# Quantised attention: turned weights as levels by VectorE, and the value products with a constant column left out

## What is computed

```
def _fq(x, delta, zp, n_bits):
    xi = _round_ste(x / delta) + zp
    xq = jnp.clip(xi, 0.0, 2.0 ** n_bits - 1.0)
    return (xq - zp) * delta

def _attn(x, ctx, wq, wk, wv, wo, bo, dq, dk, dv, dw):
    q, k, v = ...                       # x @ wq, ctx @ wk, ctx @ wv, split into heads
    sim = jnp.einsum('bhid,bhjd->bhij', _fq(q, dq, 128.0, 8), _fq(k, dk, 128.0, 8)) * SCALE
    attn = jax.nn.softmax(sim, axis=-1)
    out = jnp.einsum('bhij,bhjd->bhid', _fq(attn, dw, 0.0, 8), _fq(v, dv, 128.0, 8))
    return out.transpose(0, 2, 1, 3).reshape(b, n, D) @ wo + bo

h1 = _ln(x, ln1_g, ln1_b)
x = _attn(h1, h1, a1_wq, ..., d_w1) + x
h2 = _ln(x, ln2_g, ln2_b)
x = _attn(h2, context, a2_wq, ..., d_w2) + x
h3 = _ln(x, ln3_g, ln3_b)
a, g = jnp.split(h3 @ ff_w1 + ff_b1, 2, axis=-1)
x = a * jax.nn.gelu(g, approximate=False) @ ff_w2 + ff_b2 + x
```

## Time and profile before

| | |
|---|---|
| median of 3 runs | 2011.68 us (2011.1 to 2012.37) |
| profiled execution | 2007.97 us |
| its span | 2006.2 us |
| PE busy | 1808.6 us, 90% of the span |
| PE weight loads busy (beside PE) | 1344.1 us, 67% |
| DVE busy | 1237.6 us, 62% |
| ACT busy | 1074.7 us, 54% |
| POOL busy | 905.3 us, 45% |
| mean granted clock of PE | 0.933 |

### The profile page before, as it was taken

The page is one execution under the profiler, slowest core; times in us unless marked ns, Lnnn a source line. Parts: engine busy times, 40 slices in busy tenths (PEclk is TensorE's granted clock), DMA queues, the critical chain, the costliest instruction groups (busy, mean ns, idle before and its releaser), DMA issues.

```text
span 2006.2 us, 34807 instructions
## 1 busy us (share of the span) xinstructions
PE 1808.6 (90%) x12481; PEld 1344.1 (67%) x12481; DVE 1237.6 (62%) x2220; ACT 1074.7 (54%) x3142; POOL 905.3 (45%) x1209
## 2 busy tenths in 40 slices
PE   4998988789799889889999999999999999999997
PEld 4887876466566656657667677676676676766766
DVE  5899995744654464463575665865746647365471
ACT  2232225665575475565575564655645656565662
POOL 4466554654463363363254443644444333333340
PEclk8999998788878878879999999999999999999999
DMA  7200000002000000000002000000000000000000
GB/s 226 92 11 6 11 6 6 1 7 90 1 6 6 1 6 6 0 6 7 1 7 90 1 7 6 7 7 1 7 6 2 12 1 7 22 7 1 12 1 11
DMA packets 31073, 35.66 MB, mean 18 GB/s; under 512 B 3164, under 2 KB 29752, under 8 KB 30520
## 3 DMA queue, kind: packets, MB, share of 16 engines
q1 hardware_dynamic: 30904, 33.44, 5.2%
HBM read 31.34 MB, written 2.10 MB: 17 GB/s over the span
## 4 chain that ended last, share of the span: by engine, by line
PE 61%; DVE 17%; ACT 10%; issue 6%; POOL 2%; SPq 2%; DMA 1%; DVEq 0%; POOLq 0%; ACTq 0%
PE ps L594 33%; PE ps L806 6%; PE ps L744 6%; PE ps L816 5%; PE ps L850 4%; ACT work L983 3%; ACT work L990 3%; DVE work L1183 3%; DVE xn L1037 2%; PE ps L607 2%; DVE rowmax L1187 2%; PE ps L831 2%; ACT hT L899 1%; PE ps L766 1%; POOL work L1376 1%
## 5 line engine op out<-in xcount | busy, mean ns | idle before, releaser
L594 PE MATMUL ps<-hT,w_slot 128*128 128x256 f32 x1696 | 410.1, 396 | 17.1 <-ACT hT L899 16.1
L1300 POOL TENSOR_TENSOR work<-KT,own_head 128x512 f32<-128x512 f32 x256 | 262.4, 1046 | 285.4 <-PE ps L806 179.9
L594 PEld LDWEIGHTS ps<-hT,w_slot 128*128 128x128 f32 x1696 | 323.5, 196 | 77.2 <-ACT hT L899 21.7
L990 ACT ACTIVATE work<-work,rowmax 128x128 f32<-128x128 f32 x768 | 244.9, 391 | 167.8 <-DVE rowmax L1187 167.0
L816 PEld LDWEIGHTS ps<-ident,work 128*128 128x128 f32 x1536 | 200.1, 153 | 170.0 <-issue 90.4
L983 ACT ACTIVATE work<-ps,rowmax,score_scale 128x128 f32<-128x128 f32 x512 | 229.3, 484 | 118.7 <-DVE rowmax L1191 118.3
L816 PE MATMUL ps<-ident,work 128*128 128x128 f32 x1536 | 266.4, 302 | 17.9 <-ACT work L990 17.0
L806 PE MATMUL ps<-work,QT 128*128 128x512 f32 x512 | 266.4, 605 | 10.0 <-POOL work L1300 4.9
L1376 POOL TENSOR_SCALAR work<-work,winv 128x128 f32<-128x128 f32 x512 | 185.0, 382 | 167.7 <-DVE winv L1203 165.3
L1217 DVE RECIPROCAL O<-ps 128x128 f32<-128x128 f32 x128 | 122.3, 955 | 174.6 <-PE ps L850 173.9
L976 ACT ACTIVATE work<-ps 128x512 f32<-128x512 f32 x256 | 150.7, 596 | 91.4 <-PE ps L816 91.2
(11 more groups left out here) (131 smaller groups left out, 3170.3 us busy)
## 6 DMA issues: line engine op xcount, KB each, us to landing
ctx_in<-in_ctx SPq DMA_DIRECT2D x32, 256.0 KB, 2.7
w_slot<-in_L_xattn_W SPq DMA_DIRECT2D x2, 1024.0 KB, 6.2
w_slot<-in_L_xattn_ff_w SPq DMA_DIRECT2D x1, 2048.0 KB, 11.5
w_slot<-in_L_xattn_ffn_w SPq DMA_DIRECT2D x2, 1024.0 KB, 9.8
w_slot<-in_L_xattn_w SPq DMA_DIRECT2D x2, 1024.0 KB, 10.0
out<-x_all SPq DMA_DIRECT2D x8, 256.0 KB, 2.1
x_all<-in_x SPq DMA_DIRECT2D x1, 1536.0 KB, 11.4
pad<-in_mask_Bx1x1xS_fk SPq DMA_DIRECT2D x1, 1024.0 KB, 7.6
```

Of the source, the lines that this page charges most:

```text
L594: mm = pe.matmul(dst, lhsT(k), rhs(k), start=(k == 0 and not onto), stop=(k == chunks - 1 and not more))
L990: ex = act.activation(prob[i % NPF][:, tok(h)], src[:, tok(h)], ACT.Exp, bias=shifts[:, at:at + 1])
L1300: pool.tensor_tensor(KB[u % NK].rearrange("p (h k) -> p h k", h=HU), keys, own_head[:, e:HC:2].unsqueeze(2).broadcast_to([P, HU, S]), ALU. ...
```

## The change

The copy of a turned tile goes from ACT's queue to DVE's, and computes another thing: `min(x, MAGIC + 255) - MAGIC`, the level itself and not its complement. With levels the products with the constant column are not needed, so `values` has four products instead of eight, and `out_scale` has no minus sign. The two constants `top` and `below` go with their two memsets at the start. ACT's steps in the quantised phase now hold exponentials alone; nothing in the other layers changes.

```diff
@@ -823,13 +821,12 @@ values(u), PE
-                    for n in range(4):
+                    for e in range(2):
                         for x in range(2):
-                            pair, e = u % UJ * 2 + x, n % 2
+                            pair = u % UJ * 2 + x
                             at = pair % 4 * 32
-                            rhs = below[:, :].broadcast_to([P, S]) if n < 2 else PTb[u % 2][:, tok(2 * x + e)]
-                            mm = pe.matmul(bank(4 + j)[at:at + 32, m * S:(m + 1) * S], Vzb[st][:, j, pair, 2 * e:2 * e + 2, :], rhs,
-                                           start=(n == 0), stop=(n == 3))
+                            mm = pe.matmul(bank(4 + j)[at:at + 32, m * S:(m + 1) * S], Vzb[st][:, j, pair, 2 * e:2 * e + 2, :],
+                                           PTb[u % 2][:, tok(2 * x + e)], start=(e == 0), stop=(e == 1))
                     mm.then_inc(s["o_ps"], 1)
@@ -964,16 +961,11 @@ step(i), ACT
-                    if 0 <= u < U:
-
-                        act.wait_ge(s["o_ps"], U * ap + u + 1 - (2 if quant else 4))
+                    if not quant and 0 <= u < U:
+
+                        act.wait_ge(s["o_ps"], U * ap + u + 1 - 4)
                         act.wait_ge(s["PT_ps"], U * ap + u + 1)
-
-                        if quant:
-
-                            act.activation(PTb[u % 2], bank(2 + u % 2), ACT.Relu, bias=top[:, 0:1], scale=-1.0).then_inc(s["PT_ready"], 1)
-                        else:
-                            act.activation(PTF[u % 4], bank(2 + u % 2), ACT.Copy).then_inc(s["PT_ready"], 1)
+                        act.activation(PTF[u % 4], bank(2 + u % 2), ACT.Copy).then_inc(s["PT_ready"], 1)
@@ -1203,6 +1195,12 @@ DVE
+                def levels(u):
+
+                    dve.wait_ge(s["o_ps"], U * ap + u + 1 - 2)
+                    dve.wait_ge(s["PT_ps"], U * ap + u + 1)
+                    dve.tensor_scalar(PTb[u % 2], bank(2 + u % 2), MAGIC + 255.0, MAGIC, ALU.min, ALU.subtract).then_inc(s["PT_ready"], 1)
+
@@ -1223,6 +1221,8 @@ step(i), DVE
                     if quant and 0 <= i - SUM_LAG < U and (i - SUM_LAG) % 2:
                         inverses((i - SUM_LAG) // 2)
+                    if quant and 0 <= i - lag < U:
+                        levels(i - lag)
 
                     u = i - lag - 1
                     if quant and 0 <= u < U and u % UJ == UJ - 1:
@@ -1250,7 +1250,7 @@ tables(), DVE
-                    dve.tensor_scalar(out_scale[:, n:n + 1], deltas[:, 4 * n + 2:4 * n + 3], deltas[:, 4 * n + 3:4 * n + 4], -1.0,
+                    dve.tensor_scalar(out_scale[:, n:n + 1], deltas[:, 4 * n + 2:4 * n + 3], deltas[:, 4 * n + 3:4 * n + 4], 1.0,
```

More of the change, by code:

```diff
@@ L304, in program @@
         winv = sb("winv", [P, 2, 2 * HU])
-        top = sb("top", [P, 1])
-        below = sb("below", [P, 1], BF16)
         oinv = [[o[:, n // 2, n % 2 * P:(n % 2 + 1) * P] for n in range(U // 2)] for o in O]
@@ L1404, in _ @@
             pool.memset(neg_half[:, :], -0.5)
-            pool.memset(top[:, :], MAGIC + 255.0)
-            pool.memset(below[:, :], -255.0)
             pool.memset(ones_pair[:, 0:4:3, :], 1.0)
```

## The result

The changed kernel takes 2016.39 us (median of 8 runs, 2015.19 to 2017.62). In the same comparison the kernel before takes 2010.22 us (8 runs, 2007.16 to 2013.53). The ratio is 1.0031, with a 95% interval from 1.0021 to 1.0042, so the change costs about 6 us. The forecast was 2022 us, 10 us above the runs shown and 10.8 by the sum: the direction came, in a bit more than half the size.

The account below looks back on a forecast made before the run. PE was busiest but taken not to bound the close handovers, where VectorE is late. Eight pairs of +1.96 (close) and -0.61 us (network) give +10.8 us, so a median of 2022 us, range 2004 to 2032.

Parts of the forecast that it names:

- The close handover: Where the next phase's keys, queries and values come during this phase's last tiles (eight of 16): VectorE's queue adds 1.7 us.
- the 7.72 us gap: VectorE's idle time before the addition into x_all, after the network: tile 7's copy falls into it and adds nothing.
- The output products: Behind each close handover: clock down more often after the longer wait, 0 to 1.2 us, taken as 0.25.
- the worst case: Rival: clock falls at every close handover ahead of the output products, 1.2 instead of 0.25 us; 2030 us, chance 0.12.
- the copies of tiles 4 and 5: Close handover, before Q's and V's first operations: copies fill VectorE's idle gaps; 0.1 us, bounds 0 to 0.4.
- tile 0's before xn: Copy of tile 0 just ahead of xn on VectorE, in all 16 phases: 0 to 0.21 us, taken as 0.1.
- the low tiles: Tiles 1 and 2, at PE's low clock: omitted value products save 0.19 us a phase, the lower bound of 0.19 to 0.38.
- The phases with the network behind: The eight phases followed by a feed-forward network: 0.1 us added, 0.71 saved by omitted products, -0.61 us each.
- PE bounds the layer: Rival: the 19.5 us of omitted products come through, close handovers cost only the excess over PE's work; 1999 us, chance 0.14.
- No change: Rival: right signs, wrong sizes; a handover costs 0.8 instead of 1.8 us, low tiles credited fully; 2012 us, chance 0.17.
- The copy of 0.43 us: Rival, the skill's first rule: VectorE's copy takes 0.43 instead of 0.75 us, sum 5.7 us; 2017 us, chance 0.04.
- ScalarE's relief: 128 copies of 0.688 us leaving ScalarE, costed at nothing; 0.01 given to faster for an unseen effect.

Follow-up runs that it names:

- e3c: Changed kernel with the copies of tiles 6 and 7 back on ScalarE (no cap at 255) in the eight close phases only; 1997.90 us, 0.9943 of before.
- e4: Changed kernel with one more VectorE copy, into a spare buffer, ahead of tile 7's copy in the eight close phases; 2025.32 us, 1.0080 of before.
- e5: Changed kernel with one more VectorE copy ahead of tile 7's copy in the eight phases with the network behind; 2015.46 us, 1.0027 of before.
- e8: Changed kernel with four unused products on PE before tile 6's value products in the eight close phases; 2012.50 us, 1.0013 of before.
- e2: Kernel before with only the copy moved to VectorE, all eight products a tile kept; 2019.61 us, 1.0055 of before.
- e2b: Second run, for another profile, of the kernel before with only the copy moved to VectorE, eight products kept; 2016.10 us, 1.0038 of before.
- e1: Changed kernel with all copies back on ScalarE as levels (no cap at 255), four products a tile; 2001.32 us, 0.9960 of before.
- e3: Changed kernel with the copies of tiles 6 and 7 back on ScalarE (no cap at 255) in every phase; 1999.67 us, 0.9951 of before.
- e7: Changed kernel with eight unused products on PE before tile 6's value products in the eight close phases; 2022.79 us, 1.0064 of before.
- e6: Tiles 0 to 3 as in the changed kernel, tiles 4 to 7 as before (ScalarE complements, eight products), cap kept everywhere; 2001.67 us, 0.9957 of before.

## Why the prediction was right, and where not

**Its mechanism held.** The close handover is lost to two copies in DVE's queue between V's quantising and OT. I gave that 1.7 us; V's third to OT grew by 1.57, and OT to the exponential by 0.04. e3c removes it and e4 adds to it one for one. e5 shows that the same copy elsewhere costs nothing, as the 7.72 us gap said.

**The output products were under-sized.** I took 0.25 us of a range from 0 to 1.2. The piece from the first exponential to the turn of xn grew by 0.51. The prediction took the duration 2.90 of the earlier trace rows for a likely one; the trace has 3.10 to 3.78. Within the eight phases the piece follows it: with output products of 3.10 us it took 9.87 (nothing lost), with 3.68 us 10.60. So up to about 3.1 us the slack behind them holds, and the worst case, a fall at every handover, came about, at less than half the price that I had worked out for it. e8 shows the cause, since there the clock is kept up and the piece is back at 9.85. That the clock fell at all eight is more than the wait alone fixes: with waits of 1.90 to 2.06 us it fell at 12 of 16 handovers of e2 and e2b.

**What was over-sized, at the close handover.** I had 0.1 us for the copies of tiles 4 and 5 and 0.1 for tile 0's before xn. K to Q did grow by 0.24 us, but Q to V and V to V's third shrank by 0.19 and 0.27, the last because V's second operation takes 0.61 us on average instead of 0.88; together -0.22 and not +0.1. Why that operation is shorter is not shown. Tile 0's copy cost nothing (the 9.87 us phase has it). For the low tiles I had a saving of 0.19; the turn to K shrank by 0.03. The whole close phase came to +1.87 us against +1.96 by the sum. That it comes so near is partly luck: the output products were 0.26 us under and tile 0's copy with the low tiles 0.06 under, the copies of tiles 4 and 5 were 0.32 over and the 1.7 of the handover 0.09 over.

**The phases with the network behind hold a term that the sum left out.** The sum had -0.61 us for each, -0.48 up to the network's output and -0.13 after it; the trace has -0.31 and -0.65, -0.96. So the durations gave less than I credited, and of the -0.65 tile 7's products are only 0.11. The other 0.54 is a row that I read only as a warning: the output products at 2.90 us in the earlier trace rows. In before they ran at a low clock after this handover too, for 1.99 to 3.45 us, and in the changed kernel they take 1.99 at all six:

```profile
625.27 1.99 PE L592 MATMUL ps<-w_slot,hT 128*128 128x256 f32 x8
629.94 1.99 PE L592 MATMUL ps<-w_slot,OT 128*128 128x256 f32 x8
```

The prediction looked for a falling clock only where it added a wait, and took the phases without an added wait to change by durations alone. In the eight kernels in which all tiles leave out the products with the constant column (the changed one, e1, e3, e3c, e4, e5, e7, e8) the output products take 1.99 us at 45 of these 48 handovers and 2.68 to 2.75 at the other three; before, at one of six. So with the products out these phases run nearly always at the full clock, wherever the copy is made. The kernels that keep products there lie between: 1.99 us at five of six in e2, two of six in e2b, four of six in e6. What in the order of PE's work keeps the clock up was not tested.

**The total.** The forecast of +10.8 us was 8 x 1.96 - 8 x 0.61, 15.7 less 4.9. The layer's time grew by 9.1: the close phases gave 15.0, the durations of the others -2.7 (the 0.2 of the layer's start counted in), and the clock in six of them -3.2 (6 x 0.54). So the sum was over by 0.7 in the first, over-credited the second by 2.2, and had nothing for the third; the last two errors offset each other in large part, and that is luck. The step from 9.1 to the profiled 7.2 lies outside the layer, and the other 1 us to the 6.2 between the medians is inside the spread of before's own runs, 2007 to 2013.5.

**The rivals.** That PE bounds the layer falls with e1 (8 us, and not 19.5). No change falls by the interval. The copy of 0.43 us falls by its row, 682 ns. By the Trainium skill, "VectorE: DVE Perf Modes", section "Why PSUM operands drop a tier", f32 out of PSUM stays at the plain rate; the row agrees. The worse case, a fall of the clock at every close handover, came about in the trace, but at 0.51 us and not 1.2. ScalarE's relief, to which I gave 0.01, shows as 0.3 us (layer's time 650.1 us in e1, 649.8 in e3c).

**The marks that I had named.** The copies come twice in a row behind V's third operation, and the network's phases are shorter, as said, though by 0.96 us and not by half a microsecond. PE does not wait some 2 us twice: it waits 2.41 us for tile 6's copy and then 0.31 for tile 7's, since the second copy ends 0.6 us after the first. VectorE has 73 us more, not 90 to 96: 128 copies of 682 ns are 87, and added up one by one DVE's records have grown by 86; the busy time counts the overlap of records that follow each other directly only once. PE has 10 us less, not 14 to 17, because some of its work now runs at the low clock: e3c has the same products, its output products at 1.99 us, and 19.8 less (1788.8).

## What to carry to other kernels

Before moving an operation to a less busy engine, look up what stands behind it in that engine's queue at each place, and who waits for that: here 112 of 128 moved copies were free and 16 cost more than everything else gained. Where a wait is added for TensorE, count the work behind it at the lower clock as well, and look at the phases to which no wait is added, for their clock may change too. The best kernel was the move with those 16 left out (e3c, 1997.90 us), but its gain is that of the products: with all copies left on ScalarE the layer takes as long. e3c leaves out the cap in 16 tiles; e6 keeps it everywhere and takes 2001.67 us. Both beat the kernel before and the change.

## What the runs showed of the hardware

- An idle TensorE mostly makes later work dearer than the wait itself shows: in the changed kernel waits of 1.91 to 2.41 us were followed by output products of 3.10 to 3.78 us instead of 1.99 at all eight close handovers. In e2 and e2b, with waits of 1.90 to 2.06 us, that was so at 12 of 16, and at four they took 1.99. Filling 1.89 us of the gap with products nobody uses (e8) brought 1.99 back at all eight handovers, and the kernel became 0.18% faster by the ratios (1.0013 against 1.0031).
- Copying 128x512 f32 from PSUM to bf16 takes 682 ns on VectorE as min and subtract with immediates, and 688 ns on ScalarE. The two-operation tensor_scalar with scales from SBUF, which writes f32, takes 745 ns from the same source.
- An f32 product of 128x256 is recorded as two instructions: e8's four appear as 8 in 1.89 us, and e7's eight as 16 in 3.62.
- One program's traces can differ in pieces that no edit touches: turn to K is 8.69 us in e2 and 7.91 in e2b, and the part of the program outside the layer takes 1343.7 to 1349.5 us over the twelve traces.
